# Third bf16 part of the rotated queries and keys: made on GpSimd instead of VectorE

## What is computed

```
x = x + attention(layernorm(x))          # causal, 16 heads of 16, 4 key/value heads, rotary
x = x + cross_attention(layernorm(x), context)
x = x + ffn(layernorm(x))                # ternary weights
```

```
q  = (x @ Wqa @ Wqb).reshape(b, s, H, D)          # rank 64
kv = (x @ Wkva @ Wkvb).reshape(b, s, KVH, D, 2)   # rank 32
q = _rope(q);  k = _rope(k)
scores = einsum('bqhd,bkhd->bhqk', q, k) * scale
```

## Time and profile before

| | before |
|---|---|
| device time, median of 3 runs | 1348.08 us |
| the profiled execution: device time / span | 1350.23 us / 1348.4 us |
| first phase, until the next one's first DMA | 0 to 154.80 us |
| busy in the whole span | PE 78%, PE weight loads 56%, DVE 58%, ACT 49%, POOL 32% |
| busy in the first 154.8 us | DVE 107.5, PE 87.7, ACT 48.2, POOL 46.4 us |
| mean granted PE clock, share of 2.4 GHz | 0.79 in the first phase, 0.92 behind it |

### The profile page before, as it was taken

One profiled execution on the slowest core, in us unless ns is written; L12 is line 12 of the kernel. 1 busy time (PEld: TensorE's weight loads), 2 busy tenths in 40 slices (PEclk: granted clock), 3 DMA queues, 4 the chain that ended last, 5 costly groups with the idle time before them and its releaser, 6 DMA issues. The chain is left out here.

```text
span 1348.4 us, 22433 instructions
## 1 busy us (share of the span) xinstructions
PE 1046.7 (78%) x6749; PEld 751.9 (56%) x6749; DVE 788.7 (58%) x1680; ACT 663.5 (49%) x1166; POOL 425.9 (32%) x556
## 2 busy tenths in 40 slices
PE   3777058788999985783566989899898999988875
PEld 2444023343444433672454877778687786867764
DVE  3888356576777743863444655746656574655523
ACT  1334115565666673461225466473655747465433
POOL 0344226566333331110422231524313242330301
PEclk9677558999999996896777999999999999999987
DMA  2332423333222103257202040301203030020000
GB/s 85 103 116 74 124 92 111 114 120 105 90 96 93 58 31 135 117 223 287 57 26 84 1 125 0 109 16 44 81 0 116 8 108 16 0 78 1 10 7 16
DMA packets 52716, 103.72 MB, mean 77 GB/s; under 512 B 6640, under 2 KB 32496, under 8 KB 48560
## 3 DMA queue, kind: packets, MB, share of 16 engines
q1 hardware_dynamic: 49484, 95.53, 21.0%
q0 software_dynamic: 1920, 6.03, 1.4%
q10 hardware_dynamic: 1252, 1.39, 0.3%
HBM read 62.96 MB, written 39.58 MB: 76 GB/s over the span
## 5 line engine op out<-in xcount | busy, mean ns | idle before, releaser
L804 ACT ACTIVATE p_probs<-p_psS 128x512 f32<-128x512 f32 (+1 forms) x352 | 180.8, 563 | 122.3 <-ACTq L803 120.0
L706 DVE CUSTOM_DVE_ANT_0 p_psA<-p_psA,p_mask 128x512 f32<-128x512 f32 (+1 forms) x256 | 155.5, 647 | 103.9 <-DVEq L704 103.6
L1771 DVE TENSOR_TENSOR p_hl<-p_h,p_hh 128x512 fp32r<-128x512 f32 x128 | 86.9, 688 | 153.1 <-DVEq L1770 151.1
L838 PE MATMUL p_psA<-p_ks,p_qs 96*128 96x512 bf16 (+3 forms) x512 | 144.1, 317 | 37.0 <-PEq L836 36.7
L857 PE MATMUL p_psS<-p_qs,p_ks 99*128 99x256 bf16 (+3 forms) x512 | 131.1, 310 | 20.0 <-PEq L882 11.4
L1656 ACT ACTIVATE p_h<-p_psG,w_columns 128x512 f32<-128x512 f32 x128 | 88.3, 690 | 94.4 <-ACTq L1655 94.0
L725 POOL TENSOR_SCALAR_AFFINE_SELECT p_probs<-p_probs 128x512 f32<-128x512 f32 x128 | 80.8, 635 | 130.8 <-POOLq L724 113.8
L1975 PE MATMUL p_psY<-p_n,p_hh 128*128 128x256 f32 x512 | 105.3, 289 | 12.5 <-PEq L2035 7.6
L868 PE MATMUL p_psO<-p_probs,p_v 128*32 128x512 f32 (+3 forms) x1024 | 92.8, 457 | 26.6 <-PEq L864 25.2
L857 PEld LDWEIGHTS p_psS<-p_qs,p_ks 99*128 99x128 bf16 x512 | 44.0, 98 | 106.8 <-issue 91.8
L1697 ACT ACTIVATE p_hh<-p_h 128x512 fp32r<-128x512 f32 x64 | 40.4, 632 | 118.8 <-ACTq L1696 118.8
(11 more groups left out here) (244 smaller groups left out, 2811.6 us busy)
## 6 DMA issues: line engine op xcount, KB each, us to landing
p_n<-n_parts SPq DMA_DIRECT2D x16, 1024.0 KB, 6.8
o_sums<-p_o SPq DMA_DIRECT2D x32, 256.0 KB, 2.9
n_parts<-p_nh SPq DMA_DIRECT2D x8, 1024.0 KB, 3.9
n_parts<-p_nl SPq DMA_DIRECT2D x8, 1024.0 KB, 6.0
q_parts<-p_part SPq DMA_DIRECT2D x48, 128.0 KB
p_qs<-q_parts SPq DMA_DIRECT2D x32, 192.0 KB
p_x<-in_x_dram SPq DMA_DIRECT2D x8, 512.0 KB, 4.2
p_qs<-q_parts SPq DMA_DIRECT2D x32, 128.0 KB
```

Of the source, the lines that this page charges most:

```text
L706: nc.vector.tensor_tensor_reduce(out=bank[:, 0:w], in0=bank[:, 0:w], in1=mask[:, S - w:S], scale=1.0, scalar=MASKED, op0=ALU.add, op1=ALU.max,
L804: nc.scalar.activation(probs[:, g % 2, at:at + n * w], psS[place(s, turn) % SB][:, 0:n * w], ACT.Exp, scale=SCALE).then_inc(exp_done, 1)
L838: last = nc.tensor.matmul(bank[:, z * w:(z + 1) * w], qs[0:SROWS, k, g * G + r0 + z, i * P:(i + 1) * P], ks[0:SROWS, k, g, 0:w], start=Tru ...
L1771: nc.vector.tensor_tensor(hl[:, s, :], h[:, s, :], hh[:, s, :].bitcast(F32), ALU.subtract).then_inc(h_parts, 1)
```

## The change

The subtraction that makes the third part moves from DVE's list into POOL's. DVE's `pair` loses its third clause and so a step at the end. POOL's `pair` gets three more steps: in step s it does rot of unit s as before, and behind it part2 of unit s-3. Operands, semaphores, ACT, PE and SP stay as they are; there are as many DMAs as before.

```diff
             def pair(ahead):
-                for step in range(RING + 3):
+                for step in range(RING + 2):
...
-                    if 2 <= step < RING + 2:
+                    if step >= 2:
...
-                    if step >= 3:
-                        n = step - 3
-                        rows = P if n % UNITS < 2 else KW
-                        dve.wait_ge(mid_ready, 1)
-                        dve.sem_inc(mid_ready, -1)
-                        nc.vector.tensor_tensor(part[2][0:rows, n], rem[0:rows, n], part[1][0:rows, n],
-                                                ALU.subtract).then_inc(parts_ready, 1)
...
             def pair(ahead):
-                for step in range(RING):
-                    rows = P if step % UNITS < 2 else KW
-                    pool.wait_ge(turned, 1)
-                    pool.sem_inc(turned, -1)
-                    nc.gpsimd.tensor_tensor(rot[0:rows, step], xc[0:rows, step], xs[0:rows, step], ALU.add).then_inc(rot_ready, 1)
+                for step in range(RING + 3):
+                    if step < RING:
+                        rows = P if step % UNITS < 2 else KW
+                        pool.wait_ge(turned, 1)
+                        pool.sem_inc(turned, -1)
+                        nc.gpsimd.tensor_tensor(rot[0:rows, step], xc[0:rows, step], xs[0:rows, step], ALU.add).then_inc(rot_ready, 1)
                     if ahead and step < 2:
                         rsqrt(step)
+                    if step >= 3:
+                        n = step - 3
+                        rows = P if n % UNITS < 2 else KW
+                        pool.wait_ge(mid_ready, 1)
+                        pool.sem_inc(mid_ready, -1)
+                        nc.gpsimd.tensor_tensor(part[2][0:rows, n], rem[0:rows, n], part[1][0:rows, n],
+                                                ALU.subtract).then_inc(parts_ready, 1)
```

## The result

The changed kernel takes 1355.12 us (median of 20 runs, 1351.41 to 1360.47), the kernel before beside it 1349.9 (20 runs, 1346.21 to 1355.38). The ratio is **1.0034**, 95% interval 1.0020 to 1.0048: +4.6 us, between 2.7 and 6.5. The forecast was 1349.3 with a range of 1346.2 to 1353.2, that is +1.2 us and "no change". It was **wrong**: the kernel is slower, clear of the noise, and 1355.12 lies 1.9 us above the range. Most of these 1.9 us are the yardstick: the kernel before had a median of 1348.08 in the 3 runs that the forecast started from and of 1349.9 in 20, and the ratio put on 1348.08 gives 1352.7, inside the range. What has to be explained is +4.6 us where +1.2 was forecast.

What follows compares the result with a forecast made beforehand. The prediction took one path into SBUF, shared by DVE and POOL, and the end of rot 5 to bound each first-phase pair. Three middle pairs at 0 plus +1.2 us in the last took 1348.08 to 1349.3 us, range 1346.2 to 1353.2.

Steps and rivals of the forecast that it cites:

- 3 x 0 + 1.2 = +1.2 us: First phase: three middle pairs at 0 each plus the last pair's +1.2 us, taken as the whole kernel's change.
- A middle pair, 0: First phase, three pairs with a next one: end of rot 5 moves -0.3 or +0.2 us, taken as 0.
- Order of turns: First phase, SBUF path shared by DVE and POOL: whoever has waited longer for it goes first.
- the tie at 84.05: Second pair: rem 3 and POOL's subtraction 1 ask together; rot 5 ends at 87.02 or, rem 3 first, 87.53; before 87.30.
- The price, 1.29 us: One third-part subtraction on POOL in the first phase costs 1.29 us, like rot; its bf16 input adds nothing.
- dear: Rival: POOL's subtraction takes 1.9 us, 0.61 more each; total +6.7 us, 1354.8; chance 0.08.
- cheap: Rival: POOL's subtraction takes 0.62 us; total -4.8 us, 1343.3; chance 0.04.
- The last pair, +1.2: First phase's end: unit 2's third part done at 142.73 instead of 141.55, delaying SP's stores and phase end 1.2 us.
- POOL keeps the path: Rival: POOL holds the path between two own instructions; rem 3 follows rot 5, 0.85 us per middle pair; +4.6; chance 0.20.
- DVE wins each turn: Rival: DVE goes first on the shared path, 0.7 us gained per middle pair; total -1.0 us, 1347.1; chance 0.12.
- The PE clock: Rival: granted clock shifts between first-phase pairs, 1.8 us per pair, 3.6 for two; 1352.9 (chance 0.05) or 1345.7 (0.04).

Runs made afterwards that it cites:

- number 5: The changed kernel once more, unaltered, timed beside the kernel before on another chip: 1355.5 us, 1.0021.
- 15: The changed kernel with 104 empty instructions behind POOL's part of the first phase alone: 1353.75 us, 1.0007.
- 16: The kernel before with 104 empty instructions behind DVE's part of the first phase alone: 1354.53 us, 1.0009.
- number 14: The changed kernel with 128 empty instructions behind both DVE's and POOL's part of the first phase: 1357.14 us, 1.0031.
- 4: The changed kernel with the last pair's third parts made on DVE again: 1352.05 us, 1.0013 to the kernel before.
- 6: The changed kernel with 24 empty instructions behind DVE's part of the first phase: 1354.03 us, 1.0010.
- 7: The changed kernel with 24 empty instructions behind DVE's and 104 behind POOL's part of the first phase: 1352.86 us, 1.0005.
- 8: The kernel before with 104 empty instructions behind DVE's and 24 behind POOL's part of the first phase: 1352.71 us, 1.0017.
- 11: The changed kernel with POOL's third parts all behind rot 5 in the three pairs with a next one, last pair's on DVE: 1346.91 us, 0.9966.
- 9: The kernel before with DVE's third parts put behind step 5 in the three pairs with a next one: 1341.93 us, 0.9930.
- 3: The kernel before with a stall of about 1.2 us behind the last store of the first phase: 1352.59 us, 1.0017.
- number 13: The kernel before with a 0.38 us memset between two empty DVE instructions in each round of the last phase: 1359.43 us, 1.0053.

## Why the prediction was wrong

- **The step that failed** is the sum itself: "3 x 0 + 1.2 = +1.2 us. The profiled execution's 1350.23 becomes 1351.4". It adds up the first phase alone and takes it that phases whose instructions aren't edited keep their time. Four phases by themselves differ by 0.6 us in all; the whole kernel loses 4.6. In the traces 1.84 us of it (1.95 in number 5) are one pause of DVE in the last phase, with a fall of PE's clock behind it; the pause came there because later instructions stand elsewhere in DVE's stream. No rival held this.
- **A middle pair, 0**: right, by the mechanism that was named. Xn took 3.19 us, rot 5 ended 0.01 us from where it had in each of the three pairs.
- **Order of turns.** The replay left the tie at 84.05 open. In the trace rem 3 went first, but rot 5 came 0.0 late, not +0.2. The rule of the Trainium skill that was weighed ("SBUF — State Buffer", "Who interferes with whom": issue order decides) disagrees with this row too: POOL's subtraction was taken up at 81.73 and DVE's rem at 81.77, and rem ended in 0.68 us while POOL's lasted 1.73.
- **The price, 1.29 us**: 1.14 to 1.21 where nothing else wanted the path. The bf16 input costs nothing; the rivals "dear" and "cheap" fell.
- **The last pair, +1.2**: the third part of unit 2 came 0.83 us late, and of that 0.20 reached the phase's end. The term was mis-sized, because SP's issues behind it were reckoned with their old duration and took 0.56 us less. Whether what does reach the end costs just itself is not shown.
- **POOL keeps the path** (slower, 1352.7) gave a total nearer to the result, but its mechanism didn't occur: rem 3 never stood behind rot 5, and the second and third pair were 0.36 and 0.17 us longer, not 0.85. **DVE wins each turn** didn't occur either.
- **The PE clock** was a rival with one change in sight, between the first phase's pairs. In the profiled execution it was better there (0.78 for 0.69 in the first pair). What mattered was a drop 650 us later.

**What stays open.** With the pause at 1.9 and the phase at 0.2 or less, some 2.5 of the 4.6 us have no place; the interval of the measurement reaches down to 2.7 in all. The timed runs do not separate pause from no pause as cleanly as the traces: numbers 15 and 16 have it and were timed at +0.9 and +1.2, number 14 hasn't its full cost and was at +4.2. There is one trace for each kernel, and whether the clock falls at the gap may differ from one execution to the next. On average the six kernels with the pause ahead of the gap were timed at +2.7 us, and numbers 4, 6 and 7 without it at +1.3. Put back in its places on one or both engines the changed kernel was at +0.7 to +1.3, in its own places at +4.6, +2.8 and, with the 128, +4.2, and the intervals overlap. Which share belongs to POOL's stream wasn't settled. Nor was why DVE stops at such a place.

## What to carry to other kernels

When a transfer of work from one engine to another frees an engine that is not the bound, look for what the two share: here third parts gained nothing on either engine while rot was running, and were worth 7.9 us a phase when they were put behind it on the engine they were on. When a small change costs time in phases that it does not touch, compare the traces instruction by instruction for the place where the offset steps, and move the streams with empty instructions before blaming the edit; below some 0.3% of this kernel an edit and its side effect on places cannot be told apart without it.

## What the hardware showed that was not expected

DVE stands still for 0.35 to 0.37 us without a wait, seen once in the last phase of a trace. It goes on at 805.5 us in the changed kernel, at 801.0, 812.4 and 808.7 in numbers 8, 14 and 16, at 795.8 and 794.4 in numbers 4 and 11, and at the very end in the kernel before and in numbers 6, 7 and 9. Where it stands moved when only empty instructions were added some 650 us earlier. Counted in the rows of DVE's stream, with a loop's instructions once, it is at place 831 in the changed kernel and in numbers 4, 5, 11 and 15, at 959 in numbers 8, 14 and 16, and at 1215 in the kernel before and in numbers 6, 7 and 9. These places are 128 and 256 apart, and the 128 empty instructions of number 14 left it at the same instruction, 128 places on. In numbers 3 and 13 none was found. That is an observation on three places; the cause of the pause stays open.

Ahead of the matmuls in this round a gap of PE of 1.64 us left the granted clock at 1.00. One of 1.96 to 2.01 us was followed by a drop to 0.50 in five kernels, and in the changed kernel the 0.32 us more of gap cost 1.5 more; but one of 1.99 in number 14 and two of 1.91 in number 13 were not, while one of 1.88 was. What decides between them is not shown.
